# A three-layer graph convolution on one core: 20 instead of 17 node tiles aggregated densely in layers 1 and 2, another first source tile, and the placing of a group in two float32r parts

## The reference

```python
norm = dinv[src] * dinv[dst]
def conv(h, W, b):                       # three times, with W1 b1, W2 b2, W3 b3
    msg = (h @ W)[src] * norm[:, None]
    return segment_sum(msg, dst, 6250) + b
out = layernorm(x + conv(conv(conv(x, W1, b1), W2, b2), W3, b3))
```

## Time and profile before

| what | us |
|---|---|
| median of 3 runs (2435.20 to 2436.20) | 2435.48 |
| the profiled execution, its own time | 2434.21 |
| its span, first to last instruction | 2431.6 |
| layer 0, from its first gather | 138 to 1066 |
| layer 1 | 1066 to 1733 |
| layer 2 | 1733 to 2432 |

### The profile page before, as it was taken

One profiled execution on the slowest core, in us unless ns is written; L12 is line 12 of the kernel. 1 busy time (PEld: TensorE's weight loads), 2 busy tenths in 40 slices (PEclk: granted clock), 3 DMA queues, 4 the chain that ended last, 5 costly groups with the idle time before them and its releaser, 6 DMA issues.

```text
span 2431.6 us, 31766 instructions
## 1 busy us (share of the span) xinstructions
PE 2021.9 (83%) x9884; PEld 1063.7 (44%) x9884; DVE 1397.5 (57%) x3559; ACT 757.8 (31%) x1479; POOL 1698.9 (70%) x1780
## 2 busy tenths in 40 slices
PE   6565777888879888879999999999799999999864
PEld 6321222343434333335555555555255555555421
DVE  8425665666667665444445444445555656566677
ACT  0601333333334333232323323323323333333221
POOL 0257777777777777747777777777577777777772
PEclk7666998999999999999999999999899999999977
DMA  7656887888888888857888888889788888888894
GB/s 271 232 156 194 249 243 233 244 239 240 243 249 266 270 264 244 254 164 234 245 246 243 244 254 265 265 261 296 214 245 253 255 257 257 270 273 286 274 308 161
DMA packets 278770, 599.37 MB, mean 246 GB/s; under 512 B 65811, under 2 KB 118992, under 8 KB 278608
## 3 DMA queue, kind: packets, MB, share of 16 engines
q0 software_dynamic: 139536, 456.33, 62.1%
q1 hardware_dynamic: 139072, 141.06, 17.5%
HBM read 531.77 MB, written 65.45 MB: 246 GB/s over the span
## 4 chain that ended last, share of the span: by engine, by line
PE 19%; POOL 18%; issue 8%; DVE 6%; DMA 5%; DVEq 1%; ACT 1%; SPq 0%; ACTq 0%
POOL ring L955 18%; PE ps L1283 12%; PE ps L1169 4%; DMA ring<-y_dram,kept 2%; DMA out_dram<-row_sb 2%; PE ps L1180 2%; DVE acc L1892 1%; DVE ln L1947 1%; DVEq L1888 1%; DVE h_sb L1938 1%; DVE y_words L1938 1%; DVE h_sb L1945 1%; DVE y_words L1945 0%; ACT wide_a L1523 0%; DVE acc L2092 0%
## 5 line engine op out<-in xcount | busy, mean ns | idle before, releaser
L955 POOL DMA_INDIRECT ring<-y_dram,kept x1734 | 1672.8, 965 | 594.6 <-issue 517.8
L1169 PE MATMUL ps<-ring,onehot 128*32 128x512 f32 x3468 | 494.5, 637 | 161.5 <-DMA ring<-y_dram,kept 160.4
L1283 PE MATMUL ps<-dense_first,wide_a 128*128 128x512 f32 x1700 | 502.3, 417 | 31.4 <-ACT wide_a L1523 17.5
L2092 DVE SCALAR_TENSOR_TENSOR acc<-ps,acc 128x512 f32<-128x512 f32 x442 | 305.3, 691 | 325.5 <-PE ps L1283 315.7
L1283 PE MATMUL ps<-dense_next,wide_a 128*128 128x512 f32 x1224 | 373.4, 414 | 40.4 <-ACT wide_a L1523 31.2
L1283 PEld LDWEIGHTS ps<-dense_first,wide_a 128*128 128x128 f32 x1700 | 319.2, 193 | 198.7 <-issue 78.2
L1523 ACT CAST wide_a<-onehot 128x512 fp32r<-128x512 uint8 (+1 forms) x442 | 258.1, 594 | 354.4 <-PE ps L1283 348.0
L1283 PEld LDWEIGHTS ps<-dense_next,wide_a 128*128 128x128 f32 x1224 | 225.1, 189 | 175.2 <-issue 71.0
L1865 DVE TENSOR_TENSOR onehot<-ps,kept 128x128 f32<-128x128 f32 x438 | 125.5, 287 | 226.1 <-PE ps L1169 225.6
L1892 DVE SCALAR_TENSOR_TENSOR acc<-ps,mask,acc 128x512 f32 x294 | 207.2, 746 | 78.7 <-issue 72.9
L1169 PEld LDWEIGHTS ps<-ring,onehot 128*32 128x32 f32 x3468 | 75.1, 110 | 344.4 <-issue 325.9
(11 more groups left out here) (279 smaller groups left out, 1621.6 us busy)
## 6 DMA issues: line engine op xcount, KB each, us to landing
ring<-y_dram,kept POOLq DMA_INDIRECT x1734, 4.2
onehot<-a_dram SPq DMA_DIRECT2D x408, 64.0 KB
y_dram<-acc SPq DMA_DIRECT2D x99, 256.0 KB, 10.1
a_dram<-ring SPq DMA_DIRECT2D x17, 784.0 KB, 5.6
acc<-in_x_dram SPq DMA_DIRECT2D x1, 12288.0 KB
y_dram<-acc SPq DMA_DIRECT2D x12, 1024.0 KB, 11.0
out_dram<-row_sb SPq DMA_DIRECT2D x48, 256.0 KB
w_sb<-in_x_dram SPq DMA_DIRECT2D x24, 256.0 KB
```

The costliest lines, as they stand in the source:

```text
L955: pool.indirect_dma_start(ring[:, s, :], None, y_dram[layer], bass.IndirectOffsetOnAxis(ap=rows, axis=0)).then_inc(done, 16)
L1169: mm = pe.matmul(ps[k * WIDE:(k + 1) * WIDE, g % BANKS, :], wide_hot[:, r, k, :], ring[:, r * CPQ + k, :], start=opens, stop=closes, tile_ ...
L1283: mm = pe.matmul(ps[:, bank, :], wide_a[:, n % WIDE_SLOTS, P * k:P * (k + 1)], y_parts[(TILES * (layer - 1) + tile) % YSLOTS][:, part, :], ...
L2092: dve.scalar_tensor_tensor(out=rows, in0=ps[:, DENSE_BANKS[n % 2], :], scalar=0.5, in1=rows, op0=ALU.mult, op1=ALU.add).then_inc(dense_add ...
```

## The change

DENSE goes from 17 to 20. For the first 20 tiles 26 groups of edges fall away in layers 1 and 2 where 22 did before, so each of these layers gathers 470 chunks in 119 quads and 40 groups (518, 131 and 44 before). The units go from 221 to 260 a layer: 20 in the first block, then in layer 1 240 over quads 2 to 112, in layer 2 220 over quads 2 to 94 and 20 over 21 quads from quad 95 on. Layer 0 builds 320 windows where it built 272. The first source tile of layers 1 and 2 is tile 20, so the first block reads a tile that isn't dense.

The placing of a group is split as the dense sources are: ACT copies the sums to `high_slots` (one buffer where `slots` had two), DVE subtracts it from the bank into `low_slots` (`split_slots`, a new operation over 512 columns at the end of the group's last quad), and PE places with two float32r matmuls that add up in the bank. PE waits for `slots_split` where it waited for `slots_copied`, and the copy waits until the group before is placed.

```diff
-DENSE = 17
+DENSE = 20
-FIRST_SOURCE = 16
+FIRST_SOURCE = 20
...
+        place_part = sb("place_part", [P, 2, P], F32R)
+        high_slots = sb("high_slots", [P, D], F32R)
+        low_slots = sb("low_slots", [P, D], F32R)
...
                 if opens and g >= BANKS:
-                    pe.wait_ge(slots_copied, g - BANKS + 1)
+                    pe.wait_ge(slots_split, g - BANKS + 1)
...
                 pe.wait_ge(place_ready, g + 1)
-                pe.wait_ge(slots_copied, g + 1)
+                pe.wait_ge(slots_split, g + 1)
                 if g > 0:
                     pe.wait_ge(added, 2 * g)
-                pe.matmul(ps[:, PLACE_BANK, :], place_hot[0:rows, g % 2, :], slots[0:rows, g % 2, :],
-                          start=True, stop=True).then_inc(placed, 1)
+                pe.matmul(ps[:, PLACE_BANK, :], place_part[0:rows, g % 2, :], high_slots[0:rows, :], start=True, stop=False)
+                pe.matmul(ps[:, PLACE_BANK, :], place_part[0:rows, g % 2, :], low_slots[0:rows, :],
+                          start=False, stop=True).then_inc(placed, 1)
...
                 act.wait_ge(summed, QUADS_TO[g])
-                if g >= 2:
-                    act.wait_ge(placed, g - 1)
-                act.copy(slots[0:rows, g % 2, :], ps[0:rows, g % BANKS, :]).then_inc(slots_copied, 1)
+                if g > 0:
+                    act.wait_ge(placed, g)
+                act.copy(high_slots[0:rows, :], ps[0:rows, g % BANKS, :]).then_inc(slots_copied, 1)
...
+            def split_slots(g):
+                rows = LAST_ROWS if own_of(g) == GROUPS - 1 else P
+                dve.wait_ge(slots_copied, g + 1)
+                dve.tensor_tensor(low_slots[0:rows, :], ps[0:rows, g % BANKS, :], high_slots[0:rows, :].bitcast(F32),
+                                  ALU.subtract).then_inc(slots_split, 1)
...
                     for tile in splits_at(layer, q):
                         low_part(layer, tile)
+                    if n + 1 == QUADS_TO[g]:
+                        split_slots(g)
```

More of the change, by code:

```diff
@@ L323, in gcn_three_layers_resnorm @@
         y0_rows = sb("y0_rows", [P, 4, D], F32R)
-        sb("below_dense", [P, STORE_QUADS * CPQ * P - y_words], F32)
+        hots_at = RING_QUADS * CPQ * WIDE
+        slots_at = hots_at + 2 * P
+        sb("wide_hots", [P, hots_at], F32)
+        place_part = sb("place_part", [P, 2, P], F32R)
+        high_slots = sb("high_slots", [P, D], F32R)
+        low_slots = sb("low_slots", [P, D], F32R)
+        sb("below_dense", [P, STORE_QUADS * CPQ * P - y_words - slots_at - 2 * D], F32)
         dense_last = sb("dense_last", [P, y_words], F32R)
@@ L403, in gcn_three_layers_resnorm @@
         assert LINE + FAR <= b_at
-        hots_at = RING_QUADS * CPQ * WIDE
         wide_hot = small[:, 0:hots_at].rearrange("p (q c n) -> p q c n", q=RING_QUADS, c=CPQ)
-        place_hot = small[:, hots_at:hots_at + 2 * P].rearrange("p (b n) -> p b n", b=2)
-        slots_at = hots_at + 2 * P
         slot_place = lo_f[:, CHUNKS:CHUNKS + GROUPS]
         assert CHUNKS + GROUPS <= COLS
-        slots = small[:, slots_at:slots_at + 2 * D].rearrange("p (b d) -> p b d", b=2)
         spare_at = slots_at + 2 * D
@@ L548, in gcn_three_layers_resnorm @@
         slots_copied = sem("slots_copied")
+        slots_split = sem("slots_split")
         place_ready = sem("place_ready")
@@ L1870, in stage_group @@
                 own = own_of(g)
-                dve.tensor_scalar(place_hot[:, g % 2, :], iota_ps, slot_place[:, own:own + 1], None,
+                dve.tensor_scalar(place_part[:, g % 2, :], iota_ps, slot_place[:, own:own + 1], None,
                                   ALU.is_equal).then_inc(place_ready, 1)
@@ L2144, in first_layer @@
                         low0(k)
+                    if q + 1 == QUADS_TO[g]:
+                        split_slots(g)
             def last_tiles(layer):
```

## The result

| | median us | lowest to highest | runs |
|---|---|---|---|
| before | 2435.34 | 2434.33 to 2436.20 | 4 |
| changed | 2485.44 | 2483.61 to 2487.05 | 4 |

The ratio is 1.0206 (95%: 1.0188 to 1.0223). The time lies in the range, the sign is as forecast, and the loss is 50 us instead of 27.

A forecast was written before the change was run, and what follows sets the result against it. The prediction took POOL's gathers to set the pace before the change and PE to bound layers 1 and 2 after it. Layers 0, 1 and 2 gave 6 - 25 + 47 = +28 us on 2434.2: 2462 us, range 2430 to 2490.

The forecast's parts named there:

- PE becomes the bound in layers 1 and 2: Steady part of layer 1: PE needs 588 us, POOL's gathers 555; POOL waits for PE by tens of us in layers 1 and 2.
- The prices: PE's time in layers 1 and 2: 1.82 us a unit, 1.21 a quad's sum, 0.455 a split placing instead of 0.87.
- Layer 0, forecast +6: Layer 0: more one-hots and splits on DVE and matmuls on PE, mostly covered by slack; +6 us, 0 to +25.
- The rival of DVE's one-hots: Layer 0 becomes bound by DVE's one-hots, +25 us instead of +6, 2481 us in all; chance 0.15.
- Layer 1, forecast -25: Layer 1: steady part -31.5, third-unit waits +3, finishing dense tiles +7, after the last unit -6, first block +2.7 us.
- 3 us where a third unit waits ... and the end ... 7 us: Layer 1: 3 us of third units waiting for a group's addition, 7 us for 20 dense tiles finishing over 10 quads.
- Layer 2, forecast +47: Layer 2: steady part +25, first block +2.7, three more tiles at the end +16.3, eight splits there +3 us.
- 13 x 1.15 + 8 x 2.35 = 34 us: Layer 2, quads 2 to 94: PE's waits behind norms, 1.15 us in 13 two-unit quads, 2.35 in eight three-unit quads.
- the prices carried layer 2 of the kernel before: Kernel before, layer 2, quads 2 to 106: PE's prices and waits sum to 525 us, against 536 in the trace.
- The waits behind norms that are covered: DVE reaches the units' additions in time, so layer 2's 34 us go: 2428 us; chance 0.12, half true 0.10.
- POOL as the bound: POOL's gathers still bound layers 1 and 2, so 60 us go from each: 2344 us; chance 0.04.
- The end stretched further (+15): End of layer 2: tiles at 7 us and placings waiting for splits, +15 us more, 2477 us; chance 0.1.

The follow-up runs named there:

- experiment 4: The changed kernel without the four low-part matmuls of each dense unit in layers 1 and 2: 2348.37 us, ratio 0.9633.
- experiment 3: The changed kernel with the norm of a tile that ends at a placing begun one quad later in layer 2's steady part: 2449.55 us, ratio 1.0053.
- experiment 2: The kernel before with only 20 dense tiles and first source tile 20, the placing still in float32: 2497.07 us, ratio 1.0251.
- experiment 1: The kernel before with only the placing split in two float32r parts, 17 dense tiles and first source tile 16: 2439.34 us, ratio 1.001.
- Experiment 6: The changed kernel with ACT scaling a finished tile ahead of widening the next quad's units: 2478.41 us, ratio 1.0185.
- experiment 5: The changed kernel with two row buffers in turn for layer 2's normalised tiles: 2475.7 us, ratio 1.0165.
- experiment 7: The kernel before with the norm begun one quad later in layer 2's steady part, nothing else: 2433.7 us, ratio 0.9998.
- 5 to 8: Experiments 5, 6 and 7, and the changed kernel with 18 tiles, late norm, two row buffers and scaling first: the last 2407.44 us, ratio 0.9886.
- experiments 9 to 12: Third chip, changed kernel: 19, 17, 20 tiles with late norm, two row buffers, scaling first: 0.9938, 1.0017, 0.989; 18 tiles without these: 1.0001.
- experiment 12: The changed kernel (20 tiles) with late norm, two row buffers and scaling first, on the third chip: 2795.27 us, ratio 0.989.
- experiment 10: The changed kernel with 17 tiles, first source tile 16, late norm, two row buffers and scaling first, third chip: 2827.65 us, ratio 1.0017.

## Why the prediction was right in its sign and short by nearly half of the loss

**PE becomes the bound in layers 1 and 2: right.** By its waits for gathers (47.3 us in layer 1, then none), by POOL's waits (14.0, then 171.5), and by experiment 4, which moved nothing but PE's work and took 137 us off. The Trainium skill, Perfetto Trace Analysis, Identifying the Most-Contended Engine, says to judge TensorE's headroom by MFU and the busy share of the weight loads. The second doesn't agree with these runs: the share was 52% before, and three more tiles used up more than all the room. MFU was not worked out here.

**The prices: right.** Unit 1.82, sum 1.21 and placing 0.455 us give each undisturbed quad of experiment 3 to 0.01 us, and the placing in experiment 2 over 37 quads.

**The wait for `slots_split`, forecast at nothing: right in the steady parts.** The waits view of the whole changed span has PE waiting for the split four times, 9.1 us, and none of these stands in a steady part of layer 1 or 2.

**Layer 0, forecast +6: measured +7.4.** The windows alone gave +2.3 (experiment 2), the splits alone +2.6 (experiment 1); both are within the scatter of this layer, so that the forecast came this close is in part luck. The rival of DVE's one-hots didn't come.

**Layer 1, forecast -25: measured -14.** The first block gave +3.2 (forecast 2.7), the rest after the last unit -7.0 (forecast -6). The steady part gave -10.2 instead of -21.5. PE's own work of 588 us is as priced; the step that was mis-sized is "3 us where a third unit waits ... and the end ... 7 us". Where 10 us were forecast the trace has 15.5 us of waits, and the clock adds 3.5: it is 0.91 in the stretch from 1674 and 0.83 in the last ten microseconds, and each microsecond at a clock of 1 - x is taken to lose x, as in the unit shown above. 588 + 15.5 + 3.5 = 607 of 609.3. Experiment 6 gives back 5 of them.

**Layer 2, forecast +47: measured +59.2.** The end was right: +17.8 where +19.3 was forecast, and with the mechanism as told (5.5 us a tile through the row buffer; experiment 5). Its two terms erred in opposite ways: the tiles alone gave +13.3 (experiment 2) where 16.3 was forecast, the splits alone +5.2 (experiment 1) where 3 was, half of eight splits of 0.7 us. The first block cost 0.8 instead of 2.7. The step that was mis-sized is the steady part, "13 x 1.15 + 8 x 2.35 = 34 us", +25 forecast and +40.5 measured. The waits were 21, as counted, with 37.2 us, so this term was short by 3: the eight in quads with three units took 18.7 us (forecast 18.8), the other thirteen 18.5 (forecast 15), since seven of them last 1.68 us and not 1.13. What failed is that they were taken for the only loss, at a full clock throughout: 527 + 37.2 + 1.3 for a low part + 8.8 from the clock = 574.3 of 576.4 us. The largest part of what was missed is the clock. The clock's share is read in stretches of 20 us: four at 0.91, one at 0.94, one at 0.98, so 4 x 1.8 + 1.2 + 0.4. That these waits draw the clock's loss with them is shown by experiment 3, which took out 34.9: 27.1 of the waits (23.8 put down to DVE, 3.3 to the widening) and 8.8 of the clock make 35.9.

**That the prices carried layer 2 of the kernel before said less than it seemed.** They gave 525 of 536 us with 24 waits of 27.6 us behind norms. The trace has these 24, with 31.6 us, and 4.4 us of waits for gathers: 498 + 31.6 + 4.4 = 534. As an account of PE's time the sum was right. As an account of what sets the time it was not, as experiment 7 shows: PE's sum and the gathers' pace (105 quads in 536 us, 5.1 each) lay together there, and when the waits went, waits for gathers took their place.

**The rivals.** The waits behind norms that are covered: no, 35 us came out when they were moved. POOL as the bound: no. The end stretched further (+15): no, it came out 1.5 us under the forecast.

In all: +7.4 - 14.0 + 59.2 = 52.6 us, and with layer 0's first gather 0.6 us sooner this is the span's 51.8 but for rounding. Of the 24 us that the forecast missed, 11 are in layer 1, 12 in layer 2 and 1 in layer 0.

## What to carry to other kernels

Before moving work from one engine to another, take the pitch of a step in which the second waits for nothing, and compare it with the first's: here 4.74 against 5.0 us in layer 2, so by these prices there was room for one tile at most. An edit that frees an engine off the path (the placing in experiments 1 and 2, the late norm in 7 and 3) may measure as nothing and still be worth its price once the balance is moved, so try it again together with the move. When waits are priced, price what the clock does after them too. And where a view puts a wait down to one engine, look at where the wait stands before counting it: here four, and in the kernel before fifteen, of the waits behind norms stood under another name.

## What the runs showed of the hardware that was not expected

**The clock after short waits of PE.** Eight waits of PE for DVE of 2.1 to 2.7 us stand in the steady part of the changed kernel's layer 2. Right after five of them (1849, 2033, 2054, 2221 and 2259 us) the clock was lower, after three (1810, 1830 and 2202) it wasn't, and nowhere else in that part was it. The five make up the six stretches with a reduced clock, since one of them lies in two. In experiment 6, whose layer 2 has the same eight waits, the clock was lower after four, and not the same ones: it was lower after the first two (1800 and 1822 us), after which it stayed full in the changed kernel. A stretch with such a wait and one without, in 20 us each:

```profile
2024.00:2044.00 20.00, 17.32 (x78) 10.31 (x77) 11.67 (x22) 5.92 (x11) 10.44 (x12) 0.91 0.62 189
...
2064.00:2084.00 20.00, 18.87 (x92) 12.81 (x91) 13.37 (x25) 7.07 (x13) 12.91 (x15) 1.00 0.88 282
```

In the unit shown above two matmuls took 1.05 us at the lower of the two levels (1.2 GHz) where they take 0.62 at 2.4 GHz, so the wait of 2.13 us cost 3.9 us in all. Why some waits had this and others not is open. In the kernel before, with waits up to 1.7 us in that part, no stretch is under 1.00. Six stretches of its layer 1, where PE waited up to 4.0 us for gathers, are at 0.91; PE had room there.

**Three chips, one 16% apart.** The kernel before took 2437 us beside experiments 1 to 4 and 2435 beside 5 to 8, on two chips, and 2823 on the third. The profiles of experiments 9 to 12 have idle time that the view puts down to "remote", of which those of the ten other kernels show none. POOL's in experiment 12:

```profile
POOL ring L962 <- remote: 208.5, 103, 5.2
```

These are 2.0 us a time. In experiment 10 it is 288.2 us in 140 times. DVE and ACT show it as well. What it is was not found out, and the kernel before has no profile on that chip.
